# Two layer normalizations moved from VectorE to ScalarE in a two-layer transformer kernel

## The reference

```python
def _layernorm(x, axis=-1, eps=1e-05):
    m = jnp.mean(x, axis=axis, keepdims=True)
    v = jnp.var(x, axis=axis, keepdims=True)
    return (x - m) / jnp.sqrt(v + eps)

x = L0_attn_x
xn = _layernorm(x, axis=-1)
x = x + _L0_attn_ref(xn, ...) + _L0_ffn_ref(xn, ...)
xn = _layernorm(x, axis=-1)
x = x + _L1_attn_ref(xn, ...) + _L1_ffn_ref(xn, ...)
return x
```

## Time and profile before

| | us |
|---|---|
| median of 3 executions | 1367.89 |
| lowest, highest | 1367.87, 1368.88 |
| profiled execution, first to last instruction (span) | 1371.5 |
| TensorE busy in it | 1209.3 (88%) |
| VectorE busy | 991.5 (72%) |
| ScalarE busy | 912.8 (67%) |
| Pool busy | 692.6 (50%) |

### The profile page before, as it was taken

The page is one execution under the profiler, slowest core; times in us unless marked ns, Lnnn a source line. Parts: engine busy times, 40 slices in busy tenths (PEclk is TensorE's granted clock), DMA queues, the critical chain, the costliest instruction groups (busy, mean ns, idle before and its releaser), DMA issues.

```text
span 1371.5 us, 28942 instructions
## 1 busy us (share of the span) xinstructions
PE 1209.3 (88%) x10216; PEld 700.1 (51%) x10216; DVE 991.5 (72%) x2378; ACT 912.8 (67%) x1233; POOL 692.6 (50%) x1093
## 2 busy tenths in 40 slices
PE   2675999999999999999999999999986999899990
PEld 1342445445454545454454545454432476799990
DVE  2163888888888988888888989888868462344545
ACT  1141777778687868777786877787773667577760
POOL 6324455554536464554545464655543345466760
PEclk9898999999999999999999999999996799999995
DMA  7323505050524416060515335060615210111118
GB/s 224 63 57 64 111 19 115 20 103 27 96 53 71 91 32 120 11 115 20 103 34 88 72 52 105 19 120 14 111 37 171 74 29 25 31 48 50 50 48 250
DMA packets 80300, 100.90 MB, mean 74 GB/s; under 512 B 8800, under 2 KB 56672, under 8 KB 79776
## 3 DMA queue, kind: packets, MB, share of 16 engines
q1 hardware_dynamic: 75680, 89.85, 29.9%
q0 software_dynamic: 4480, 9.22, 2.3%
HBM read 73.50 MB, written 25.01 MB: 72 GB/s over the span
## 4 chain that ended last, share of the span: by engine, by line
PE 63%; DVE 20%; issue 5%; ACT 4%; POOL 4%; DMA 3%; ACTq 0%; SPq 0%; DVEq 0%; POOLq 0%
PE PS L628 9%; PE PS L595 8%; PE PS L440 7%; PE PS L484 7%; PE PS L561 5%; PE PS L639 4%; PE PS L580 4%; PE PS L423 4%; DVE xn L824 3%; PE PS L434 2%; DVE nm L985 2%; DMA early<-gate_rows 2%; PE PS L462 2%; PE PS L570 2%; DVE ra L933 1%
## 5 line engine op out<-in xcount | busy, mean ns | idle before, releaser
L735 ACT ACTIVATE flow<-PS 128x1024 f32<-128x1024 f32 x320 | 321.2, 1028 | 129.4 <-PE PS L580 112.1
L1146 POOL TENSOR_SCALAR_AFFINE_SELECT flow<-flow 128x256 f32<-128x256 f32 (+1 forms) x448 | 191.0, 444 | 374.3 <-ACT flow L735 371.7
L595 PE MATMUL PS<-flow 128*32 128x512 f32 (+3 forms) x2048 | 181.2, 455 | 6.2 <-POOL flow L1146 6.2
L985 DVE TENSOR_REDUCE nm<-PS 128x2 f32<-128x1024 f32 x128 | 154.6, 1220 | 42.3 <-PE PS L549 38.9
L1133 POOL TENSOR_TENSOR early<-early 128x512 f32<-128x512 f32 x128 | 160.7, 1270 | 20.9 <-DMA early<-gate_rows 20.0
L484 PE MATMUL PS<-early,down 128*128 128x512 f32 x288 | 151.8, 637 | 18.4 <-POOL early L1133 17.9
L726 ACT COPY qp<-PS 2x1024 f16<-2x1024 f16 x128 | 128.5, 1004 | 51.0 <-PE PS L570 49.8
L440 PE MATMUL PS<-xnT,up 128*128 128x512 f32 x288 | 152.6, 625 | 3.7 <-DVE at L908 3.4
L987 DVE TENSOR_REDUCE nm<-PS 128x2 f32<-128x768 f32 x128 | 121.6, 950 | 32.4 <-PE PS L549 32.3
L628 PE MATMUL PS<-xsT,w1s 128*128 128x128 f32 x1152 | 141.5, 276 | 3.0 <-DVE act L1079 2.9
L1076 DVE SCALAR_TENSOR_TENSOR tanh<-tanh,PS 128x512 f32<-128x512 f32 x72 | 49.5, 687 | 130.0 <-ACT tanh L769 130.0
(11 more groups left out here) (178 smaller groups left out, 2263.3 us busy)
## 6 DMA issues: line engine op xcount, KB each, us to landing
early<-gate_rows SPq DMA_DIRECT2D x32, 1024.0 KB, 10.8
qp<-relay_q SPq DMA_DIRECT2D x64, 128.0 KB
kp<-relay_k SPq DMA_DIRECT2D x64, 128.0 KB
xsb<-xs SPq DMA_DIRECT2D x76, 64.5 KB, 1.8
relay_k<-qkh SPq DMA_DIRECT2D x32, 128.0 KB, 2.3
early<-in_w SPq DMA_DIRECT2D x1, 4096.0 KB, 14.8
out_y<-X SPq DMA_DIRECT2D x4, 1024.0 KB, 7.9
relay_q<-qkh SPq DMA_DIRECT2D x16, 128.0 KB, 2.3
```

The source lines that it names most:

```text
L595: ins = pe.matmul(m.PS[32 * j:32 * j + 32, m.PV, kt * P:], m.vst[b % 2][:, kt, 4 * g + j, :], m.pt[:, r, k * L + o:k * L + o + L - kt * P] ...
L735: act.activation(m.pt[:, n % RING, :], m.PS[:, i:i + 2, :].rearrange("p k c -> p (k c)"), ACT.Exp, scale=1.0 / SCALE).then_inc(s["exp"], 1)
L985: dve.tensor_reduce(nm[:, 3, 2 * n:2 * n + 2], ps, AX_X, ALU.max, negate=True).then_inc(s["max"], 1)
L1146: ins = pool.affine_select(part, part, [[0, part.shape[1]], [1, P]], ALU.is_ge, nothing, base=0, channel_multiplier=-1)
```

## The change

Both normalizations go from VectorE to ScalarE. ScalarE computes scale·x + shift with a scale and a shift per partition (token): scale is `rstd` as before, and shift is -mean·rstd, which Pool computes with two more instructions of 128x4 elements after each `rstd`: a product into `ve` (semaphore `scaled`) and a multiplication by -1 into a new tile `shift` (semaphore `shift`). The places in the order stay. Pool gets one further wait: before it overwrites `rstd` it waits for the normalization of the batch before.

```diff
@@ scalar_program
+    def normalize(n, b):
+        act.wait_ge(s[f"shift{n}"], b + 1)
+        for t in range(NT):
+            ins = act.activation(m.xn[n][:, t, 0:D], m.X[:, b * NT + t, :], ACT.Identity,
+                                 bias=m.shift[:, n, t:t + 1], scale=m.rstd[:, n, t:t + 1])
+        ins.then_inc(s[f"norm{n}"], 1)
+
+    def norm0(b, i):
+        if b:
+            act.wait_ge(s["xnT0_mm"], b)
+        normalize(0, b)
+
+    def norm1(b, i):
+        if b:
+            act.wait_ge(s["xnT1_mm"], b)
+            act.wait_ge(s["d_sorted"], 16 * NT * b)
+        normalize(1, b)
@@ vector_program
-    def normalize(n, b):
-        xt = m.X[:, b * NT:(b + 1) * NT, :]
-        dve.wait_ge(s[f"rstd{n}"], b + 1)
-        for t in range(NT):
-            ins = dve.tensor_scalar(m.xn[n][:, t, 0:D], xt[:, t, :], m.mv[:, n, t, 0:1], m.rstd[:, n, t:t + 1],
-                                    ALU.subtract, ALU.mult)
-        ins.then_inc(s[f"norm{n}"], 1)
...
@@ pool_program, stats
         pool.wait_ge(s[f"var{n}"], b + 1)
+        if b:
+            pool.wait_ge(s[f"norm{n}"], b)
         pool.tensor_tensor(m.rstd[:, n, :], m.ve[:, n, :], m.neghalf[:, :], ALU.pow).then_inc(s[f"rstd{n}"], 1)
+        pool.wait_ge(s[f"rstd{n}"], b + 1)
+        pool.tensor_tensor(m.ve[:, n, :], m.mv[:, n, :, 0], m.rstd[:, n, :], ALU.mult).then_inc(s[f"scaled{n}"], 1)
+        pool.wait_ge(s[f"scaled{n}"], b + 1)
+        pool.tensor_scalar(m.shift[:, n, :], m.ve[:, n, :], -1.0, None, ALU.mult).then_inc(s[f"shift{n}"], 1)
```

More of the change, by code:

```diff
@@ L260 @@
     "max heads x2 tables rowzero silu glu chain final "
-    "fills kept ones var0 var1 rstd0 rstd1 qs gated rotated noaT spare nextspare rows xsorted spare_rows "
+    "fills kept ones var0 var1 rstd0 rstd1 scaled0 scaled1 shift0 shift1 qs gated rotated noaT spare nextspare rows xsorted spare_rows "
     "d_x d_w d_restx d_gate d_gates d_relayq d_relayk d_relayed d_sorted d_w1 d_w2 d_pad d_out"
@@ L338, in place @@
         m.rstd = sb("rstd", [P, 2, NT], where=side)
+        m.shift = sb("shift", [P, 2, NT], where=side)
         m.xn = [sb(f"xn{n}", [P, NT, D + n], where=side) for n in range(2)]
@@ L774, in outputs @@
         act.copy(m.ysb[:, n % U, :], wk(("outputs", 0, n))[:, 0:D]).then_inc(s["ycopy"], 1)
-    share = dict(xnT0=xnT0, up=up, q=q, route0=route0, gT=gT, at0T=at0T, down=down, xnT1=xnT1, parts=parts,
-                 v=v, route1=route1, mrows=mrows, score=scores, sums=sums, mT=mT, staged=staged, turned=turned,
+    share = dict(norm0=norm0, norm1=norm1, xnT0=xnT0, up=up, q=q, route0=route0, gT=gT, at0T=at0T, down=down, xnT1=xnT1,
+                 parts=parts, v=v, route1=route1, mrows=mrows, score=scores, sums=sums, mT=mT, staged=staged, turned=turned,
                  hidden=hidden, outputs=outputs)
@@ L831, in stats0 @@
         stats(0, b)
[L833 to L842, removed]
     def kvr(b, t):
@@ L1080, in hidden @@
                                  op0=ALU.mult, op1=ALU.mult).then_inc(s["glu"], 1)
-    share = dict(stats0=stats0, norm0=norm0, norm1=norm1, kvr=kvr, kv=kv, route0=route0, gate=gate, attn0=attn0, x1=x1,
+    share = dict(stats0=stats0, kvr=kvr, kv=kv, route0=route0, gate=gate, attn0=attn0, x1=x1,
                  stats1=stats1, xnT1=xnT1, logits=logits, rope=rope, parts=parts, route1=route1, expert=expert,
```

## The result

The changed kernel takes 1408.66 us (median of 4 executions, 1408.18 to 1410.49) beside 1368.39 (4 executions, 1367.87 to 1370.34) for the kernel before: a ratio of 1.029, 95% interval 1.027 to 1.030, or 40.3 us more. The forecast was 1387, so the sign was right and the loss was twice as large as worked out.

A forecast was written before the change was run, and what follows sets the result against it. TensorE, busy 58.17 of 60 us, was taken as the bound; -13.9 + 22.1 + 5.6 + 3.6 + 2 = +19.4 us on the 1371.5 us span, the median becoming 1387 us. Range for 8 in 10: 1364 to 1400; the forecast's own: 1376 to 1398.

The forecast's parts named there:

- norm0 off VectorE: In steady passes: with norm0's 3.08 us off VectorE, TensorE's 1.07 us wait for `mt` at L570 goes whole, -13.9 us.
- norm0 on ScalarE costs nothing: Between the exponentials of units 6 and 7: four activations of 1.67 us fit into 1.65 us of idle time, no cost.
- norm1 on ScalarE: Ahead of the copy to `oT` in ScalarE's queue: late `shift` and norm1 idle TensorE 1.7 us a pass, +22.1 us.
- They add nothing: Exponentials of units 12 and 13, queued behind norm1, start about 1.7 us late, as late as TensorE, so no added cost.
- nothing downstream gives it back: After TensorE's late `oT` transposition: no later slack recovers the 1.7 us a pass, since remaining waits hang on TensorE's progress.
- Pool in stats0: Pool's two instructions delay the masking TensorE awaits at L595, 0.64 us in 8 passes, 0.1 in 5: +5.6 us.
- Ramp: At the start: the first norm0 and norm1 of batches 0 and 1 each come 1.2 us later, +3.6 us.
- Relief of VectorE deciding: Rival 1: VectorE's relief decides and ScalarE keeps `oT` nearly in time, 1363 us, or 1357 without L595's wait; 12%.
- a balance: Rival 2: loss and gain cancel, with a stall of 0.6 us a pass, 1368 us; 9%.
- The slow product on Pool: Rival 3: Pool's new product takes a power's time, 0.8 us more each, +24, 1411 us; 6%.
- The stall spreads: Rival 4: ScalarE is also late with masking inputs and the transposed norm1's copy, 0.7 us more a pass, 1396 us; 11%.

The follow-up runs named there:

- reordered kernel: The changed kernel with norm1 placed behind the copy to `oT` in ScalarE's order instead of ahead of it: 1390.54 us, ratio 1.015 to the kernel before.
- norm0 alone: The kernel before with only norm0 moved to ScalarE and Pool's shift computed for norm0 only; norm1 stays on VectorE: 1371.08 us, ratio 1.0007.
- norm1 alone: The kernel before with only norm1 moved to ScalarE and Pool's shift computed for norm1 only; norm0 stays on VectorE: 1396.89 us, ratio 1.021.
- The filled wait: The changed kernel with 12 extra identity transpositions on TensorE just before its wait for `oT`: 1403.71 us, ratio 1.024 to the kernel before.
- the version with norm0 alone: The kernel before with norm0 on ScalarE and Pool's stats0 part moved ahead of the indirect DMAs: 1362.86 us, ratio 0.9937; with 24 idle Pool increments 1362.72, 0.9956.

## Why the prediction was right or wrong

**norm0 off VectorE: wrong, 8 us.** The step that failed is "With 3.08 us less on VectorE, `mt` comes before 432.65, so the wait goes whole". The wait fell from 1.07 to 0.62 us, 0.45 x 13 = 5.9 instead of 13.9. The three VectorE instructions before `mt` were taken at their old lengths (0.23 for L1004), as though only norm0 lay beside Pool's products. Freed of norm0, VectorE waits for TensorE's scores and comes to L1004 just as Pool starts its last product. The groups of L1004 and L1002 also give most of VectorE's missing relief: 64 instructions each, 21.2 us before and 30.4 after at L1004, 23.4 and 27.2 at L1002, 13 of the 15 us between 64 and 49. The prediction said that what is late next is TensorE itself; it was Pool's product. (Pool gained nothing from VectorE's relief: its gating products take 1267 ns in the mean after and 1270 before.) The row at 447.21 bears out a page of the Trainium skill that I did not use ("SBUF — State Buffer", SBUF: two separate sides): a VectorE instruction with two inputs in SBUF and a Pool instruction that reads SBUF take turns at a shared port, and the later one waits for the earlier one to end. L1004 has two such inputs and ended 0.09 us after Pool.

**norm0 on ScalarE costs nothing: right.** Its four activations took 1.64 us at 443.15, against 1.67 worked out, and the exponential behind them still waited 0.42 for TensorE (445.21). ScalarE's own group for the new line shows the duration of one:

```profile
L667 ACT ACTIVATE xn<-X,shift,rstd 128x128 f32<-128x128 f32 x128 | 52.5, 482 | 38.4 <-POOL shift L1122 38.4
```

482 ns; the estimate was 492 from rows. The other one, 479 by the Trainium skill ("ScalarE: Activation LUTs", What ACT_TABLE_LOAD costs), was the closer.

**norm1 on ScalarE: the mechanism and its size right.** Pool's product took 0.20 us (0.25 said), `shift` began 0.29 after it, ScalarE sat idle 0.68 before norm1, and TensorE 1.68 before the transposition of `oT` (1.7 said): 1.68 x 13 = 21.8, where +22.1 stood. The reordered kernel shows that this is the cause. Of each 1.68 us about 1.5 reach the length of a pass: an undisturbed pass after the change is 64.10 us, one with norm0 alone 62.60, one with norm1 alone 63.85 beside 62.38 before. In the tail the wait was 2.76 us, where +2 stood. The recorded range does not follow from its bounds: they give 1380 to 1397, not 1376 to 1398.

**"They add nothing", "nothing downstream gives it back": wrong, 6 us.** The exponentials behind did add nothing. But a pause of TensorE is not only its own length: in four of twelve passes the granted clock was 0.50 for some 3 us behind it, 1.6 us each, 6.3 in all. The filled wait brings this back. The steady stretch of before had no such pause, its longest was 1.07, and a granted clock of 1.00, so it gave no sign; the prediction counted idle time as a plain sum.

**Pool in stats0: undersized, 3 us.** 8 x 0.64 + 5 x 0.1 = 5.6 was said. The kernel with norm0 alone puts it at 0.67 in every pass (0.22 more in all, and 0.45 saved at `mt`), 8.7 in thirteen. That is a difference of passes and not a wait that was read: TensorE's wait for the masking grew by only 3 us in all, from 6.2 to 9.2, in that kernel. The slack of 0.55 that I had given to five passes, from what was left of a sum of waits, hid nothing.

**Ramp: right for what it named, 5 us missing.** TensorE's two waits for norm1 in the ramp grew to 4.62 and 4.71 us, each 1.2 more (the earlier trace rows has 3.41), and the first wait of all from 24.1 to 25.3: together the 3.6 that was said. The pause of Pool had no term: 5.4 us. It is no effect of what the change computes.

**The sum.** 8.0 + 6.3 + 3.1 + 5.4 = 22.8 us of missing terms. The forecast's 19.1 over the median and these make 41.9, and 40.3 were measured; the stall, of which 19.5 us reach the passes and not 22.1, is more than the difference. The forecast also let the medians differ as much as the spans, and they differ by 40.3 and 35.3: the profiled execution of before was too slow to stand for its median.

**The rivals.** Relief of VectorE deciding (1363) and a balance (1368) needed a copy late by less than 0.8 us; it was late by far more. The slow product on Pool is refuted by 0.20 us. "The stall spreads" came nearest in size (1396) with the wrong mechanism: ScalarE's later instructions were in time, and the loss spread through the clock and the start-up. That two unforeseen costs could lie on top of a right stall was in no case, and so the range ended at 1400.

## What to carry to other kernels

When work is moved between engines that take turns in order, ask first what stands behind the new place in that engine's queue: here one number in the order (norm1 behind the copy instead of before it) was worth 19 us, nearly half of the loss. Take the lengths of short VectorE instructions as valid only for the Pool instruction that they ran beside; when a stage slides, look up what it slides beside. And count a pause of TensorE as possibly more than itself: here pauses of 1.56 us and more brought the lower clock in some passes, pauses up to 1.07 never in the steady part. Keep small additions out of a queue that TensorE waits for by moving them earlier, as the version with norm0 alone does.

## What the hardware showed that I had not expected

- Pool's product beside it lengthened a 128x16 VectorE product from 0.23 to 1.18 us, and and beside its products and maskings four normalizations took 3.08 and 4.20 us instead of 1.20. Pool's own product took 1.26 or 1.27 us in all these cases.
- After a pause of 1.68 us TensorE's clock was granted at 0.50 for about 3 us in some passes and not in others, after one of 2.31 us as well; after 1.07 or 0.63 us never in the steady part of any run. What decides between the passes is open. With the 1.68 us filled it stayed at 1.00.
- Pool stood for 9 us ahead of an indirect DMA with all that it waited for done, while the DMA engines were busy, in five kernels with the new instructions for both norms, and for about 7 us in one with norm0's alone at the earlier place. With 24 idle increments ahead, or with one norm's instructions at their old place, it did not.
- On Pool a product of 128x4 takes 0.20 us and a power 1.04, so the 1.04 is the price of the function and not of starting an instruction.
